# phi(k)v in four groups of 32 columns, with a reordered start and a reordered end of each batch

## The chip, the cores and the metric

One core of one Trainium2 chip runs the whole layer in one launch. The metric is the device time in microseconds (us) of an execution. All rows below come from one profiled execution of the kernel before.

## The reference, cut to what matters

The input x is 16 sequences of 512 tokens with 256 channels. It is normalised, and the output is x + attention(xn) + ffn(xn). The change touches the linear attention:

```python
q, k, v = xn @ Wq + bq, xn @ Wk + bk, xn @ Wv + bv      # 16 heads of 16 channels
q, k = elu(q) + 1, elu(k) + 1                           # phi(q), phi(k)
kv = einsum('bkhd,bkhm->bhdm', k, v)                    # 16 x 16 for each head
out = einsum('bqhd,bhdm->bqhm', q, kv) / maximum(q . sum_k k, 1e-6)
attention = out.reshape(B, S, 256) @ Wo + bo
```

The ffn is a shared SwiGLU of 512 hidden channels plus a SwiGLU whose output goes through the two best of 8 experts of a token.

## The kernel before, in words

Work goes in 16 batches (one sequence each; the first and the last are written out, 1 to 14 are one loop), and then in 75 tiles of 128 tokens that are sorted by pair of experts (the tile stage). Products that need more than one pass are done as three matmuls of rounded high and low parts (mm3, L337 to L339: high*high, high*low, low*high); a matmul that is written once in plain f32 is run by the chip as two pairs of weight load and matmul.

A batch on TensorE (batch, L476): k and v of the four token blocks (L481 to L494), q (L498), hidden(0) of the shared ffn, then **phi(k)v** (L514 to L518), hidden(1), routed(0), the ranks of the tokens (L529, L534), the normalisers (L543), routed(1) and routed(2), the product with Wo (L558), routed(3), spread (L566), hidden(2), hidden(3), and the output sums y (L592 to L608). Waits stand between them by hand: L540 waits for gate(0) of VectorE before the normalisers, L556 for the transposed kv, L569 for the third routed gate, L593 and L600 for the low parts of the hidden values that GpSimd makes.

phi(k)v takes, for each of two chunks c of 128 channels and four token blocks t, phi(k)'s 128 columns as the stationary operand and v's 128 columns with a column of ones behind them as the moving one: 8 products of 128 x 129 of which only the 16 x 16 blocks on the diagonal are wanted. VectorE reads the column of ones as the sum of k (L966), adds bv times that sum (L973), sets all but the heads' blocks to zero with the mask head (L977), and transposes the result within blocks of 32 (L987). It is the stationary operand of L558.

The engines beside TensorE, in the order written out by hand:

- VectorE in a batch (L925): norm(b+1), base(b-1) (which adds y to the residual), k_in for four blocks with normalise(b+1) behind the second, phi_k, the expert choice in some 20 small dependent steps (probabilities, best_two), phi(q) (L960), ksum and khead, gate(0) (L971), kvm, gate(1), the ranks and table rows with routed_gate(0) among them, the transposition, routed_gate(1), the reciprocals (L993 to L1001), routed_gate(2), m_lo, routed_gate(3), qn, gate(2), qn_lo, **x_transposed(b+1, 0)**, gate(3), x_transposed(b+1, 1), t_low(b+1). In the first batch norm(1) stands at L989 and **normalise(1)** at L1006, ahead of routed_gate(2). normalise waits for a power that GpSimd takes (reciprocal_root, L1156). x_transposed waits for the reload of the normalised x (xn_ld) and for the scattered stores of the routed values (hs_st).
- ScalarE: the copy of v out of the accumulator (L689), the exponentials, the silus, the high parts (high, L676), the high part of x (t_high, L667) behind high(3).
- GpSimd: the residual's bias (L1186), the split of 1/16 of the experts' weights, low(0), low(1), four scattered stores of table rows and four of routed values (L1181), low(2), low(3) (L1162).
- SyncE issues the loads and stores; x of batch b+2 is loaded once x_transposed of b+1 is through (L373).

At the start SyncE issues x in four parts, the constants, the weights of k and v (stage_kv), then the rest. ScalarE makes high parts of stage_kv, waits for the weights of q (L734), and only then makes the high part of x (first_high, L736), then those of w_in and half of w1. GpSimd makes the low parts of w_in in cuts of 256 columns (L1234 to L1236), and the parts of w1. In the last batch VectorE also works out the list of tiles (tile_list, L1003), and SyncE stores zeros in 13 places (L409) after ends_rdy (L984) and before the first tile's loads.

Of the kernel before, what the change touches and what calls it, by code (L numbers as in the profile page):

```python
# [6 lines left out]
def layer_program(nc, x, w_k, w_v, w_q, w_o, w_in, w_out, w_exp, w_rt, b_q, b_kl, b_vo,  # L7
# [3 lines left out]
    ALU = mybir.AluOpType  # L11
# [3 lines left out]
    P = 128  # L15
    B, S, D = 16, 512, 256
# [30 lines left out]
    with ctx:  # L47
# [27 lines left out]
        v = sb("v", [P, TB, DC, P + 1], f32)  # L75
# [8 lines left out]
        stay = sb("stay", [P, 2 * P + DC * 32 + NROW + 11], f32)  # L84
        ident = stay[:, 0:P]
        head = stay[:, P:2 * P]
        heads = stay[:, 2 * P:2 * P + DC * 32].rearrange("p (c n) -> p c n", c=DC)
        crow = stay[:, 2 * P + DC * 32:2 * P + DC * 32 + NROW]
        cpart = stay[:, 2 * P + DC * 32 + NROW:]
# [10 lines left out]
        bvo = sb("bvo", [P, 2 * D], f32)  # L100
        bv, bo = bvo[:, 0:D].rearrange("p (c n) -> p c n", c=DC), bvo[:, D:2 * D]
# [9 lines left out]
        kvm = relut[:, 0, 0:DC * P].rearrange("p (c n) -> p c n", c=DC)  # L111
        kvT = relut[:, 1, 0:DC * P].rearrange("p (c n) -> p c n", c=DC)
# [235 lines left out]
        def _(sp):  # L348
# [7 lines left out]
            loads(kv_w_ld, [], stage_kv)  # L356
# [3 lines left out]
            loads(out_w_ld, [(bvo[:, :], b_vo), (wo[:, :, :], w_o)], [])  # L360
# [6 lines left out]
            def load(b, last):  # L367
# [7 lines left out]
                if first_row(b):  # L375
                    sp.wait_ge(ffn_split, 1)
                else:
                    wait_apart(sp, base_rdy, DC * b)
                    sp.dma_start(out_rows(b - 1), res[:, :, :]).then_inc(base_st, 16)
                    wait_apart(sp, base_st, 16 * b)  # L380
                sp.dma_start(res[:, :, :], x_rows(b)).then_inc(r_ld, 16)
                if first_row(b):
                    sp.wait_ge(w1_split, 1)
                    loads(out_w_ld, [], stage_out)
                    sp.wait_ge(ffn_split, 3)
                else:
                    sp.wait_ge(wexp_split, b)
# [51 lines left out]
        def _(pe):  # L439
# [36 lines left out]
            def batch(b, last):  # L476
# [28 lines left out]
                if first_row(b):  # L505
                    pe.wait_ge(ffn_split, 2)
# [81 lines left out]
                if first_row(b):  # L588
                    pe.wait_ge(ffn_split, 3)
# [62 lines left out]
        def _(act):  # L652
# [29 lines left out]
            def batch(b, last):  # L682
# [3 lines left out]
                for i in range(2):  # L686
                    act.wait_ge(v_done, 2 * b + i + 1)
                    wait(act, acc_done, b)
                    act.copy(v[:, 2 * i:2 * i + 2, :, 0:P],  # L689
                             bank[7 if i == 0 else 0][:, :].rearrange("p (t c n) -> p t c n", t=2, c=DC)).then_inc(v_rdy, 1)  # L690
# [6 lines left out]
                    act.activation(expt[:, i, :], expt[:, i, :], ACT.Exp, scale=-1.0).then_inc(ek_rdy, 1)  # L697
                act.wait_ge(lg_rdy, b + 1)
# [78 lines left out]
        def _(dve):  # L777
# [147 lines left out]
            def batch(b, last):  # L925
# [29 lines left out]
                if first_row(b):  # L955
                    dve.wait_ge(ffn_split, 2)
# [4 lines left out]
                acc = bank[2][:, 0:DC * (P + 1)].rearrange("p (c n) -> p c n", c=DC)  # L961
# [4 lines left out]
                dve.tensor_copy(ksum[:, :], acc[:, :, P]).then_inc(kstep, 1)  # L966
# [5 lines left out]
                for c in range(DC):  # L972
                    ins = dve.scalar_tensor_tensor(kvm[:, c, :], bv[:, c, :], ksum[:, c:c + 1], acc[:, c, 0:P],  # L973
# [3 lines left out]
                dve.tensor_tensor(kvm[:, :, :], kvm[:, :, :], head.unsqueeze(1).broadcast_to([P, DC, P]),  # L977
# [9 lines left out]
                dve.transpose(kvT.rearrange("p c n -> p (c n)"), kvm.rearrange("p c n -> p (c n)")).then_inc(kvT_rdy, 1)  # L987
# [17 lines left out]
                if first_row(b):  # L1005
                    normalise(1)  # L1006
# [85 lines left out]
            dve.memset(v[:, :, :, P:P + 1], 1.0)  # L1092
# [54 lines left out]
        def _(pool):  # L1147
# [30 lines left out]
            def batch(b, last):  # L1178
# [21 lines left out]
                if first_row(b):  # L1200
                    pool.wait_ge(out_w_ld, 16 * 3)
                    high_part(wstage[:, :], wout_hi_)
                    pool.wait_ge(pool_set, 4)
# [33 lines left out]
            pool.wait_ge(w1_ld, 16 * 2)  # L1237
            pool.wait_ge(w_round, len(stage_kv) + len(stage_q) + len(stage_in) + 1)
            low_part(stage_w1[0][0], stage_w1[0][2], stage_w1[0][3], w1_split)
            high_part(stage_w1[1][0], stage_w1[1][2])  # L1240
            pool.wait_ge(pool_set, 3)
            low_part(stage_w1[1][0], stage_w1[1][2], stage_w1[1][3], w1_split)
# [34 lines left out]
def constants():  # L1277
# [5 lines left out]
    head = (p[:, None] // 16 == p[None, :] // 16).astype(np.float32)  # L1283
# [62 lines left out]
```

## Time and profile before

| what | us |
|---|---|
| three timed runs: median (lowest to highest) | 950.98 (949.29 to 952.27) |
| the profiled execution, its own time | 949.65 |
| its span, first to last instruction | 947.8 |
| TensorE matmuls busy in the span | 920.9 |
| VectorE, GpSimd, ScalarE busy | 703.4, 471.0, 362.6 |

The span leaves 1.85 us of the execution's time outside it. The profiled execution is 1.3 us below the median of the runs. Batches 1 to 14 repeat with a period of about 43.3 us; the tile stage begins at 723.2 us. Matmuls overlap in their pipeline, so a row's duration is longer than what the matmul costs; the distance between two starts is the cost.

### The profile page before, as it was taken

Reading aid. Unit: us, or ns where it says so; the run is one execution under the profiler, and the core shown is the slowest. Engines: PE = TensorE matmul, PEld = TensorE weight load, DVE = VectorE, ACT = ScalarE, POOL = GpSimd, SP = SyncE. Lnnn points to the kernel's source line nnn. Section 1 sums busy time; section 2 is a strip of 40 time slices with the busy share of each in tenths; the row PEclk is TensorE's granted clock in tenths of the full one; section 3 lists DMA queues with packets and bytes.
Section 4 is the critical chain, followed back from the end, with each engine's and each line's share of the span. In section 5 each row is a group of like instructions: output and inputs, shape, how many; then the busy total and the mean of one; then the engine's idle time right before and its main releaser. Section 6 shows DMA issues by size and latency. Waiting matters only on the chain. (4 is left out here: it accounts for less than half of the span.)

```text
span 947.8 us, 21218 instructions
## 1 busy us (share of the span) xinstructions
PE 920.9 (97%) x6206; PEld 836.3 (88%) x6207; DVE 703.4 (74%) x1770; ACT 362.6 (38%) x595; POOL 471.0 (50%) x550
## 2 busy tenths in 40 slices
PE   7879999999999999999999999999999999999995
PEld 6778989898988989898988889898879999999995
DVE  5768687877878686877778787868495787777773
ACT  4425345353435354453434353544332222222220
POOL 4764453535253543645353534535262656665554
PEclk8989999999999999999999999999999999999998
DMA  9242323241413223232413132231235777787760
GB/s 271 67 125 87 105 72 135 67 122 46 121 67 100 89 78 117 62 134 65 122 56 111 67 100 89 78 129 44 93 132 164 145 144 142 140 147 142 136 128 1
DMA packets 145911, 100.34 MB, mean 106 GB/s; under 512 B 55520, under 2 KB 136800, under 8 KB 145888
## 3 DMA queue, kind: packets, MB, share of 16 engines
q1 hardware_dynamic: 106032, 64.76, 23.8%
q0 software_dynamic: 17968, 25.32, 12.3%
q10 hardware_dynamic: 21888, 9.97, 3.8%
q8 instruction: 12, 0.20, 0.1%
q14 instruction: 11, 0.09, 0.0%
HBM read 53.43 MB, written 48.00 MB: 107 GB/s over the span
## 5 line engine op out<-in xcount | busy, mean ns | idle before, releaser
L337 PE MATMUL bank<-wexp_hi,xnT_hi 128*128 (+1 forms) x560 | 190.9, 341 | 0.0
L339 PE MATMUL bank<-wexp_hi,xnT_lo 128*128 (+1 forms) x560 | 186.2, 332 | 0.0
L338 PE MATMUL bank<-wexp_lo,xnT_hi 128*128 (+1 forms) x560 | 185.8, 332 | 0.0
L1162 POOL TENSOR_TENSOR h_lo<-gated,h_hi 128x256 fp32r<-128x256 f32 x128 | 100.6, 805 | 124.9 <-ACT h_hi L676 124.9
L337 PEld LDWEIGHTS bank<-wexp_hi,xnT_hi 128*128 128x128 f32 x560 | 106.2, 190 | 13.1 <-issue 3.2
L339 PEld LDWEIGHTS bank<-wexp_hi,xnT_lo 128*128 128x128 f32 x560 | 106.2, 190 | 10.4
L338 PEld LDWEIGHTS bank<-wexp_lo,xnT_hi 128*128 128x128 f32 x560 | 106.3, 190 | 9.6
L337 PE MATMUL bank<-xnT_hi,win_hi 128*128 128x512 f32 x256 | 102.0, 398 | 8.5 <-DVE expt L923 8.5
L1186 POOL TENSOR_TENSOR res<-res,bvo 128x256 f32<-128x256 f32 x64 | 48.3, 785 | 115.3 <-DMA res<-x 115.3
L339 PE MATMUL bank<-xnT_hi,win_lo 128*128 128x512 f32 x256 | 100.5, 393 | 0.0
L338 PE MATMUL bank<-xnT_lo,win_hi 128*128 128x512 f32 x256 | 100.3, 392 | 0.0
L676 ACT CAST h_hi<-gated 128x512 fp32r<-128x512 f32 x64 | 39.8, 622 | 116.7 <-DVE gated L919 116.7
L338 PE MATMUL bank<-wexp_lo,h_hi 128*128 x296 | 83.3, 281 | 0.0
L337 PE MATMUL bank<-wexp_hi,h_hi 128*128 x296 | 83.1, 281 | 0.0
L1181 POOL DMA_INDIRECT tab_d<-rows,pos_i x64 | 64.2, 1003 | 37.9 <-DVE tok L915 21.3
L339 PE MATMUL bank<-wexp_hi,h_lo 128*128 x296 | 83.0, 281 | 0.0
L1259 POOL DMA_INDIRECT out<-res,idx_cur x39 | 61.5, 1577 | 39.0 <-DVE res L1116 32.0
L337 PE MATMUL bank<-wkv_hi,xnT_hi 128*128 128x266 f32 (+1 forms) x256 | 73.7, 288 | 4.8 <-DVE xnT_lo L824 4.8
L338 PE MATMUL bank<-wkv_lo,xnT_hi 128*128 128x266 f32 (+1 forms) x256 | 73.5, 287 | 0.0
L339 PE MATMUL bank<-wkv_hi,xnT_lo 128*128 128x266 f32 (+1 forms) x256 | 73.2, 286 | 0.0
L339 PE MATMUL bank<-wout_hi,h_lo 128*128 128x256 f32 x256 | 72.2, 282 | 0.0
L337 PE MATMUL bank<-wout_hi,h_hi 128*128 128x256 f32 x256 | 72.2, 282 | 0.0
(190 smaller groups left out, 2433.8 us busy)
## 6 DMA issues: line engine op xcount, KB each, us to landing
res<-x SPq DMA_DIRECT2D x16, 512.0 KB, 3.6
out<-res SPq DMA_DIRECT2D x16, 512.0 KB, 2.9
xt<-x SPq DMA_DIRECT2D x15, 512.0 KB, 3.5
xn_d<-xt SPq DMA_DIRECT2D x15, 512.0 KB, 4.8
xt<-xn_d SPq DMA_DIRECT2D x60, 128.0 KB, 3.2
xt<-h_d SPq DMA_DIRECT2D x76, 64.0 KB
xt<-h_d ACTq DMA_DIRECT2D x76, 64.0 KB
kb<-h_d SPq DMA_DIRECT2D x76, 64.0 KB
```

The costliest lines, as they stand in the source:

```text
L337: e.matmul(to, w_hi, m_hi_, start=first_, stop=False, skip_group_check=free)
L338: e.matmul(to, w_hi, m_lo_, start=False, stop=False, skip_group_check=free)
L339: return e.matmul(to, w_lo, m_hi_, start=False, stop=last_, skip_group_check=free)
L676: act.copy(h_hi[:, j, :], gated[:, j % 2, :]).then_inc(hhi_rdy, 1)
L1162: ins = pool.tensor_tensor(h_lo[:, j, cols], gated[:, j % 2, cols], h_hi[:, j, cols].bitcast(f32), ALU.subtract)
L1181: pool.indirect_dma_start(d, bass.IndirectOffsetOnAxis(ap=pos_i[:, t:t + 1], axis=0), src, None).then_inc(done, 16)
L1186: ins = pool.tensor_tensor(res[:, t, :], res[:, t, :], bo, ALU.add)
L1259: pool.indirect_dma_start(out, bass.IndirectOffsetOnAxis(ap=idx_cur[:, t // TB, t % TB:t % TB + 1], axis=0), ring[t], None, bounds_check=N ...
```

## The change

It makes phi(k)v of 4 times as many matmuls of a quarter of the width. The stationary operand is 32 columns of phi(k) (two heads), the moving one the same 32 columns of v and a column of ones, and the four groups of a chunk go to the four blocks of 32 partitions of the accumulator. kvm is then 32 wide, kvT is a tile of its own that is zero outside its diagonal blocks, and four transpositions of 32 partitions fill these. Beside that:

- the bias bv comes with the constants in the new layout, and b_vo becomes b_o;
- the weights of k and v are issued from ScalarE's queue at the start, and first_high stands ahead of the wait for q's weights;
- both high parts of w1 are made by ScalarE inside the first batch, between the exponentials of k and those of q; GpSimd makes only low parts, w_in's in cuts of 128 columns, in the order in which hidden(0) to hidden(3) need them;
- in the first batch, normalise(1) stands behind qn instead of ahead of routed_gate(2);
- in each batch, gate(3) stands ahead of both halves of x_transposed.

```diff
-        v = sb("v", [P, TB, DC, P + 1], f32)
+        v = sb("v", [P, TB, DC, QG, HP + 1], f32)          # HP = 32, QG = 4
-        kvm = relut[:, 0, 0:DC * P].rearrange("p (c n) -> p c n", c=DC)
-        kvT = relut[:, 1, 0:DC * P].rearrange("p (c n) -> p c n", c=DC)
+        kvm = relut[:, 0, 0:DC * HP].rearrange("p (c n) -> p c n", c=DC)
+        kvT = sb("kvT", [P, DC, P], f32)
...
             sp.dma_start(stay[:, :], c_stay).then_inc(stay_ld, 16)
-            loads(kv_w_ld, [], stage_kv)
...
                 if first_row(b):
-                    pe.wait_ge(ffn_split, 2)
+                    pe.wait_ge(ffn_split, 1)
...
                 for c in range(DC):
                     for t in range(TB):
-                        mm = pe.matmul(bank[2][:, c * (P + 1):(c + 1) * (P + 1)], phik[:, t, c * P:(c + 1) * P], v[:, t, c, :],
-                                       start=(c == 0 and t == 0), stop=(t == TB - 1), skip_group_check=True)
+                        for n in range(QG):
+                            at = c * P + n * HP
+                            mm = pe.matmul(bank[2][n * HP:(n + 1) * HP, c * (HP + 1):(c + 1) * (HP + 1)], phik[:, t, at:at + HP],
+                                           v[:, t, c, n, :], start=(c == 0 and t == 0), stop=(t == TB - 1), skip_group_check=True)
                 mm.then_inc(acc_done, 1)
+                if first_row(b):
+                    pe.wait_ge(ffn_split, 2)
                 hidden(1, (0, 1))
...
-                    act.copy(v[:, 2 * i:2 * i + 2, :, 0:P],
-                             bank[7 if i == 0 else 0][:, :].rearrange("p (t c n) -> p t c n", t=2, c=DC)).then_inc(v_rdy, 1)
+                    act.copy(v[:, 2 * i:2 * i + 2, :, :, 0:HP].rearrange("p t c h n -> p (t c h) n"),
+                             bank[7 if i == 0 else 0][:, :].rearrange("p (o n) -> p o n", n=HP)).then_inc(v_rdy, 1)
...
+                if first_row(b):
+                    act.wait_ge(w1_ld, 16 * 2)
+                    high_parts(stage_w1)
                 act.wait_ge(lg_rdy, b + 1)
...
+            for buf, of, _, _ in stage_kv:
+                act.dma_start(buf, of).then_inc(kv_w_ld, 16)
             act.wait_ge(kv_w_ld, 16 * 3)
             high_parts(stage_kv)
+            first_high()
             act.wait_ge(q_w_ld, 16 * 4)
             high_parts(stage_q)
-            first_high()
             act.wait_ge(in_w_ld, 16 * 2)
             high_parts(stage_in)
-            act.wait_ge(w1_ld, 16 * 2)
-            high_parts(stage_w1[:1])
...
-                    ins = dve.scalar_tensor_tensor(kvm[:, c, :], bv[:, c, :], ksum[:, c:c + 1], acc[:, c, 0:P],
+                    ins = dve.scalar_tensor_tensor(kvm[:, c, :], bv[:, c, :], ksum[:, c:c + 1], acc[:, c, 0:HP],
...
-                dve.transpose(kvT.rearrange("p c n -> p (c n)"), kvm.rearrange("p c n -> p (c n)")).then_inc(kvT_rdy, 1)
+                wait(dve, m_done, b)
+                for i in range(4):
+                    rows = slice(HP * i, HP * i + HP)
+                    ins = dve.transpose(kvT[rows, :, HP * i:HP * i + HP], kvm[rows, :, :])
+                ins.then_inc(kvT_rdy, 1)
...
                 if last:
                     tile_list()
-                if first_row(b):
-                    normalise(1)
                 routed_gate(b, 2, 1)
...
                     dve.tensor_tensor(qn[:, c, :], phiq[:, c, :], bank[(6, 2)[c]][:, :], ALU.mult).then_inc(qn_rdy, 1)
+                if first_row(b):
+                    normalise(1)
                 gate(b, 2, 1)
...
+                gate(b, 3, 7)
                 if not last:
                     x_transposed(b + 1, 0)
-                gate(b, 3, 7)
-                if not last:
                     x_transposed(b + 1, 1)
                     t_low(b + 1)
...
+            dve.memset(kvT[:, :, :], 0.0)
...
-            for n, (buf, _, hi, lo) in enumerate(stage_in):
-                pool.wait_ge(w_round, len(stage_kv) + len(stage_q) + n + 1)
-                low_part(buf, hi, lo, ffn_split)
...
+            pool.wait_ge(w_round, first + len(stage_in))
+            for j in range(HC):
+                for buf, _, hi, lo in stage_in:
+                    for at in (j * P, 512 + j * P):
+                        ins = pool.tensor_tensor(lo[:, at:at + P], buf[:, at:at + P], hi[:, at:at + P].bitcast(f32), ALU.subtract)
+                ins.then_inc(ffn_split, 1)
+            for n in range(2):
+                pool.wait_ge(w_round, first + len(stage_in) + n + 1)
+                low_part(stage_w1[n][0], stage_w1[n][2], stage_w1[n][3], w1_split)
```

## Rows read from the trace of the kernel before

**Rows 1.** The page, busy time of each engine.
```profile
PE 920.9 (97%) x6206; PEld 836.3 (88%) x6207; DVE 703.4 (74%) x1770; ACT 362.6 (38%) x595; POOL 471.0 (50%) x550
```

**Rows 2.** Timeline of TensorE around phi(k)v: start us, us, engine line op
```profile
295.90 1.95 PE L516 MATMUL bank<-v,phik 128*128 128x129 f32 x16
297.60 0.48 PE L337 MATMUL bank<-xnT_hi,win_hi 128*128 128x512 f32 x1
297.92 0.40 PE L338 MATMUL bank<-xnT_lo,win_hi 128*128 128x512 f32 x1
298.15 0.39 PE L339 MATMUL bank<-xnT_hi,win_lo 128*128 128x512 f32 x1
```

**Rows 3.** The same view around the normalisers.
```profile
303.44 0.65 PE L543 MATMUL bank<-phiq,khead 128*32 128x128 f32 x16
304.02 0.50 PE L337 MATMUL bank<-wexp_hi,xnT_hi 128*128 128x512 f32 x1
304.35 0.39 PE L338 MATMUL bank<-wexp_lo,xnT_hi 128*128 128x512 f32 x1
```

**Rows 4.** L543 in short windows: start:end us, length, PE and PEld busy (instructions), clock
```profile
303.44:303.48 0.04, 0.04 (x4) 0.04 (x6) 1.00 0.00 0
303.48:303.57 0.09, 0.09 (x4) 0.09 (x8) 1.00 0.00 0
```

**Rows 5.** Line views of TensorE's queue, one batch: when its sequencer was at L547, L550
```profile
L547 PEldq ALU_OP  x1: 32/32/32, 303.5 to 303.5; - x1
L550 PEldq ALU_OP  x1: 32/32/32, 303.7 to 303.7; - x1
```

**Rows 6.** Timeline of VectorE, same batch: fourth k_in and gate(0)
```profile
289.92 0.42 DVE L930 TENSOR_TENSOR kb<-bank,bkl 128x256 f32<-128x256 f32 x1 [0.73 <-PE bank L339]
301.85 0.68 DVE L919 TENSOR_TENSOR gated<-gated,bank 128x512 f32<-128x512 f32 x1
```

**Rows 7.** Timelines of VectorE, GpSimd and TensorE at the end of that batch.
```profile
319.96 0.71 DVE L830 STREAM_TRANSPOSE phik<-xt 128x512 f32<-128x512 f32 x1 [0.79 <-DMA h_d<-expt,pos_i]
320.60 0.65 DVE L919 TENSOR_TENSOR gated<-gated,bank 128x512 f32<-128x512 f32 x1
321.98 1.44 POOL L1162 TENSOR_TENSOR h_lo<-gated,h_hi 128x256 fp32r<-128x256 f32 x2 [1.52 <-ACT h_hi L676]
323.31 0.28 PE L339 MATMUL bank<-wout_hi,h_lo 128*128 128x256 f32 x1
323.56 0.36 PE L337 MATMUL bank<-m_hi,qn_hi 128*128 128x256 f32 x1
323.76 0.28 PE L338 MATMUL bank<-m_lo,qn_hi 128*128 128x256 f32 x1
```

**Rows 8.** Who waited for whom: us in total, times, longest
```profile
PE bank L337 <- POOL h_lo L1162: 2.6, 2, 1.8
```

**Rows 9.** Batch 14: timeline of VectorE; a window of all engines (clock 0.50)
```profile
668.32 0.71 DVE L830 STREAM_TRANSPOSE phik<-xt 128x512 f32<-128x512 f32 x1 [2.68 <-DMA h_d<-expt,pos_i]
672.30:675.70 3.40, 3.40 (x18) 3.40 (x17) 0.60 (x1) 0.00 (x0) 0.00 (x0) 0.50 0.00 0
```

**Rows 10.** The start: timelines of ScalarE and TensorE.
```profile
11.33 0.62 ACT L655 CAST wq_hi<-expt 128x512 fp32r<-128x512 f32 x1 [2.15 <-DMA relut<-c_round]
13.30 0.56 PE L337 MATMUL bank<-wkv_hi,xnT_hi 128*128 128x266 f32 x1 [4.75 <-DVE xnT_lo L824]
```

**Rows 11.** Batches 0 and 1: timelines of VectorE and TensorE.
```profile
47.92 3.02 DVE L818 TENSOR_SCALAR xt<-xt,mv,rstd 128x256 f32<-128x256 f32 x4 [4.49 <-POOL rstd L1156]
51.59 0.80 PE L337 MATMUL bank<-xnT_hi,win_hi 128*128 128x512 f32 x1 [7.15 <-DVE expt L923]
59.66 0.71 DVE L830 STREAM_TRANSPOSE phik<-xt 128x512 f32<-128x512 f32 x1 [1.14 <-DMA xt<-xn_d]
```

**Rows 12.** The last batch: SyncE's zeros, the first tile's low part.
```profile
698.66 13.97 SPq L409 DMA_DIRECT2D h_d<-wstage  x13
722.36 0.65 DVE L1089 TENSOR_TENSOR xnT_lo<-phiq,xnT_hi 128x512 fp32r<-128x512 f32 x1
```

More of the change, by code:

```diff
@@ L15, in layer_program @@
     P = 128
+    HP = 32
+    QG = P // HP
     B, S, D = 16, 512, 256
@@ L83, in layer_program @@
         NROW = 16 + 4 * NSLOT
-        stay = sb("stay", [P, 2 * P + DC * 32 + NROW + 11], f32)
+        stay = sb("stay", [P, P + 3 * HP + DC * 32 + NROW + 11], f32)
         ident = stay[:, 0:P]
[L86 to L89, printed above, removed]
+        head = stay[:, P:P + HP]
+        bv = stay[:, P + HP:P + 3 * HP].rearrange("p (c n) -> p c n", c=DC)
+        stay_at = P + 3 * HP
+        heads = stay[:, stay_at:stay_at + DC * 32].rearrange("p (c n) -> p c n", c=DC)
+        crow = stay[:, stay_at + DC * 32:stay_at + DC * 32 + NROW]
+        cpart = stay[:, stay_at + DC * 32 + NROW:]
         triones = sb("triones", [P, 2, P], bf16)
@@ L99, in layer_program @@
         bk, brt = bkl[:, 0:D], bkl[:, D:KL]
-        bvo = sb("bvo", [P, 2 * D], f32)
-        bv, bo = bvo[:, 0:D].rearrange("p (c n) -> p c n", c=DC), bvo[:, D:2 * D]
+        bo_t = sb("bo_t", [P, D], f32)
+        bo = bo_t[:, :]
         stats = sb("stats", [P, TB, 6], f32)
@@ L359, in _ @@
             loads(w1_ld, [], stage_w1)
-            loads(out_w_ld, [(bvo[:, :], b_vo), (wo[:, :, :], w_o)], [])
+            loads(out_w_ld, [(bo, b_o), (wo[:, :, :], w_o)], [])
             sp.wait_ge(fill_set, 2)
@@ L375, in load @@
                 if first_row(b):
-                    sp.wait_ge(ffn_split, 1)
+                    sp.wait_ge(ffn_split, HC)
                 else:
@@ L384, in load @@
                     loads(out_w_ld, [], stage_out)
-                    sp.wait_ge(ffn_split, 3)
+                    sp.wait_ge(ffn_split, HC + 1)
                 else:
@@ L588, in batch @@
                 if first_row(b):
-                    pe.wait_ge(ffn_split, 3)
+                    pe.wait_ge(ffn_split, HC + 1)
                 if last:
@@ L955, in batch @@
                 if first_row(b):
-                    dve.wait_ge(ffn_split, 2)
+                    dve.wait_ge(ffn_split, HC)
                 for o in range(DC):
@@ L965, in batch @@
                 dve.wait_ge(acc_done, b + 1)
-                dve.tensor_copy(ksum[:, :], acc[:, :, P]).then_inc(kstep, 1)
+                dve.tensor_copy(ksum[:, :], acc[:, :, HP]).then_inc(kstep, 1)
                 dve.wait_ge(kstep, KS * b + 1)
@@ L976, in batch @@
                 dve.wait_ge(kstep, KS * b + 3)
-                dve.tensor_tensor(kvm[:, :, :], kvm[:, :, :], head.unsqueeze(1).broadcast_to([P, DC, P]),
+                dve.tensor_tensor(kvm[:, :, :], kvm[:, :, :], head.unsqueeze(1).broadcast_to([P, DC, HP]),
                                   ALU.mult).then_inc(kvm_rdy, 1)
@@ L1202, in batch @@
                     high_part(wstage[:, :], wout_hi_)
-                    pool.wait_ge(pool_set, 4)
+                    pool.wait_ge(pool_set, 3)
                     low_part(wstage[:, :], wout_hi_, wout_lo_, ffn_split)
@@ L1232, in high_part @@
                 ins.then_inc(pool_set, 1)
-            for n, (buf, _, hi, lo) in enumerate(stage_in):
-                pool.wait_ge(w_round, len(stage_kv) + len(stage_q) + n + 1)
-                low_part(buf, hi, lo, ffn_split)
[L1237 to L1242, printed above, removed]
+            first = len(stage_kv) + len(stage_q)
+            pool.wait_ge(w_round, first + len(stage_in))
[7 more added lines that the diff above has]
+                low_part(stage_w1[n][0], stage_w1[n][2], stage_w1[n][3], w1_split)
             wout_hi_, wout_lo_ = (w[:, :, :].rearrange("p c n -> p (c n)") for w in (wout_hi, wout_lo))
@@ L1274, in _, with constants @@
                 pool.wait_ge(out_st[t], 16 * (NG if t < LAST_TILES else NG - 1))
-def constants():
+def constants(bv):
     P, D, N = 128, 256, 8192
@@ L1297, in constants @@
     part = np.stack([p * P, p] + [t * P + p for t in range(4)] + [-(p // 16 % 2)] + [p // 32 == t for t in range(4)], 1)
-    stay = np.concatenate([ident, head, heads.reshape(P, -1), crow, part], 1)
+    bv = np.repeat(bv.reshape(2, 4, 32).transpose(1, 0, 2).reshape(4, 64), 32, 0)
+    stay = np.concatenate([ident, head, bv, heads.reshape(P, -1), crow, part], 1)
     other = np.concatenate([tri, spread.reshape(P, -1)], 1)
@@ L1335 @@
         "b_kl": every(np.concatenate([a["L0_attn_bk"], a["L0_ffn_gb"], a["L0_ffn_eb"]])),
-        "b_vo": every(np.concatenate([a["L0_attn_bv"], a["L0_attn_bo"]])),
-        **constants(),
+        "b_o": every(a["L0_attn_bo"]),
+        **constants(a["L0_attn_bv"]),
     }
```

8 lines of the change are left out of this document (4 added, 4 removed).

## The prediction

> **What bounds the kernel now.** I read first the busy times: TensorE's matmuls cover 920.9 of 947.8 us, no other engine is above 74% [rows 1]. Then TensorE's own waits: where its stalls are few and long, a gain comes either from fewer matmul slots or from those few stalls [rows 8, 10, 11]. Then the timelines around phi(k)v and around the normalisers, because L543 is already a product in four groups of 32 columns and so prices the new form [rows 2 to 4]. Last VectorE's order, since an edit that makes TensorE faster runs into what VectorE delivers to it [rows 6, 7]. A slot is the distance between two starts, not a row's duration: an f32r matmul of 512 columns costs 0.23 us (297.92 to 298.15), one of 256 columns 0.12 (323.76 follows 323.56 by more, of which below).
>
> **Part 1, phi(k)v on TensorE.** Old cost: 16 pairs of load and matmul start at 295.90; the second matmul behind them starts at 297.92. That is 2.02 us, less 0.23 for the first one behind: 1.79 us in a batch, 0.11 for each pair [rows 2].
>
> New: 64 pairs of 32 stationary and 33 moving columns. L543 is 16 pairs of 32 and 128: from 303.44 to the second matmul behind at 304.35, less 0.23, is 0.68 us [rows 3]. Inside it four matmuls start within 0.04 us, then none until after 303.57 [rows 4]: the four groups run side by side, a round of four every 0.11 us, which is 256 columns (two passes of 128) at the granted full clock. Four rounds are 0.44, so leaving the mode costs 0.68 - 0.44 = 0.24, and I add 0.11, one exposed load, for entering it. With 33 columns a round is 33/128 of 0.109, 0.028 us; 16 rounds are 0.45. Floor: 0.11 + 0.45 + 0.24 = 0.80 us.
>
> The question is whether pairs come that fast (7 ns each). The queue's own rows bound it: TensorE's sequencer was at L547 at 303.5 and at L550 at 303.7, and between these lines stand the 12 pairs of routed(1) [rows 5]. So it hands over a pair in at most 17 ns. Before phi(k)v it stands some 16 pairs ahead (in those rows 12 of L543's 16 were still to start). The other 48 at 17 ns are 0.82 us: at most 0.11 + 0.82 + 0.24 = 1.17. The group saves G = 0.62 to 0.99 us.
>
> VectorE caps that. From the start of its fourth k_in, 289.92, it is busy nearly without a pause until gate(0) ends at 302.53, and none of those steps changes [rows 6]. L543 waits for gate(0) and starts at 303.44 [rows 3]; with 0.14 us from an engine's end to the matmul it releases (GpSimd's 323.42 to 323.56 [rows 7]) it can start at 302.67, 0.77 earlier and not more. I take 0.75 a batch, nearest to the cap because both ends of G straddle it. It counts from batch 1's k to batch 15's k, 14 times: **-10.5 us**. Bounds 0.35 (twice the supply time I allow) to 0.80: -5 to -11.
>
> In batch 15 the next stage hangs on VectorE: ends_rdy, then 13 stores of zeros over 13.97 us, then the first tile's loads, whose low part ends at 723.01 as TensorE arrives [rows 12]. phi(k)v is not in that path; I count 0.
>
> The copy of v, the narrower kvm and mask, and four small transpositions for one of 0.44 us stand outside the path (kvT's next reader is L558, behind routed(2)). I cost them at nothing; their cover is TensorE's routed(1) and routed(2), and if it went, the four transpositions would cost some 0.1 us a batch.
>
> **Part 2, gate(3) ahead of x_transposed.** VectorE waits for the scattered stores until 319.96, transposes, and starts gate(3) only at 320.60. Behind gate(3) come ScalarE's high(3) and GpSimd's low(3), which ends at 323.42; TensorE starts the last part of y at 323.56 where 323.43 was its slot, and the pair behind is 0.20 away, not 0.12: 0.45 us for two slots of 0.12 [rows 7]. The stall is 0.21 us in each batch. With gate(3) 0.6 us earlier it goes: 13 batches x 0.21 = **-2.7 us**. What is late next is low(2), on GpSimd behind the eight scattered stores. The transpositions end when they did, or 0.6 earlier, since gate(3) no longer lies between them.
>
> In batch 14 the stores come late, VectorE waits 2.68 us for them with gate(3) behind, TensorE stalls 1.8 us by the wait's row and 2.0 by the starts [rows 8, 9], and the clock is then at its lower level from 672.3 to 675.7, which costs half of 3.4 us [rows 9]. Both should go: -3.7; **-3.5 us** taken, since low(2) may be late too. Bounds -1.5 to -3.7.
>
> **Part 3, the start and batches 0 and 1.** TensorE waits 4.75 us for the low part of x [rows 10]. In that chain ScalarE waits 2.15 us for the load that ends q's group and makes q's high part, 0.5, ahead of x's. That goes: 2.6 us. Against it, 522 KB of weights of k and v now share the DMA engines with x's 512 KB from the first microsecond on, and x heads the chain. No row shows the mix; bounds are a gain of 4.75 (the whole wait) and a loss of 1. I take 2.0, the removed 2.6 less some delay of x.
>
> In batch 0 TensorE waits 7.15 us for routed_gate(2) behind normalise(1), which waits for GpSimd until 47.9 and takes 3.02 us [rows 11]; the clock is lower behind it (the row's 0.80 us against the usual 0.39). Moved behind qn, normalise(1) frees that gate, but it still ends at 50.9 less the start's gain, and the store and reload of the normalised x, x_transposed (59.66, waiting for the reload [rows 11]), the load of the next x, norm(2), base(0) and k_in(0) of batch 1 follow in one chain that knows nothing of TensorE. So most of the 7.15 comes back as waits for GpSimd's low parts in batch 0 and for k_in in batch 1. What stays: 2.0 of the start, 0.6 from gate(3) leaving the two transpositions, and what VectorE waited for TensorE ahead of two of batch 1's four k_in, twice about 0.73 (as [rows 6] shows for a later batch): 4.1. Some 0.6 more I take for base(0), which no longer waits for y. **-4.7 us**, bounds -2 to -7.5. Those of w1's high parts that ScalarE now makes inside batch 0 delay q's exponentials by 2 us; VectorE has the expert choice to do meanwhile.
>
> **Sum.** 10.5 + 2.7 + 3.5 + 4.7 = 21.4. Against the profiled execution's 949.65 that gives 928.3; the median of the runs stands 1.3 higher, so 929.5.
>
> **A rule against the change.** Rows: matmuls of different column groups start four in 0.04 us [rows 4]. TensorEngine Tiling (Array Packing), Instruction Overhead, in the Trainium skill says that a matmul has some 60 cycles of overhead, so that one column costs what 60 do, and that no factor should be taken from a dimension already small; 33 columns are below that. By it, as an estimate, 64 times 25 ns are 1.6 us and the group would cost 1.95, more than now. The rows of L543 do not show such a floor across groups.
>
> **Rivals.** *A, supply binds (slower).* The queue holds enough for L543's 16 pairs, so its burst may say little of 64. Place: the 48 pairs behind the first 16. If they came no faster than the slowest spacing of small pairs in these rows that isn't set by their columns, L516's own 0.11 us, the group would cost 0.35 + 64 x 0.11 = 7.4, +5.6 a batch; at 0.06 us, +2.4 a batch over 16 batches is +38, less 11 of parts 2 and 3: 978. It turns the total to slower by 0.3% above about 0.036 us a pair. For: nothing in the trace keeps up small pairs for long. Against: 17 ns between L547 and L550. TensorE: Matmul & The Clock Gate (What happens when you issue a matmul) in the Trainium skill gives 62 ns for each matmul where the sequencer's program decodes; the rows of L547 and L550 speak against it here.
>
> *B, the groups load one after another (small gain).* If 64 loads of 32 columns queue up at a quarter of L516's 0.107 us each, the group costs 0.35 + 1.71 = 2.06, +0.27 in 16 batches: 949.65 + 4.3 - 10.9 + 1.3 = 944. Against: the six loads within 0.04 us [rows 4].
>
> *C, the gain in phi(k)v is there, but parts 2 and 3 give nothing.* If x's loads are delayed as much as the wait for q saved, and batch 0's stall only moves, the time is 949.65 - 10.5 - 2.7 + 1.3 = 938.
>
> *D, nothing measurable:* the group half fast (1.8 us) and C together, about 948 to 951.
>
> **Chances.** Forecast 0.62, C 0.16, B 0.08, D 0.05, A 0.09. A measurement can tell about 0.3% (2.9 us) from no change. A and its like are slower: 0.09; D is mostly the same, 0.05; the rest faster, 0.86. Range: the forecast's terms at their bounds give 926 to 940 (5 + 2.7 + 1.5 + 2 = 11.2 less at the weak end, 11 + 2.7 + 3.7 + 7.5 = 24.9 at the strong one); this takes C in. I give 923 to 941.
>
> **What would show it.** Right: L516 as 64 narrow pairs within 0.5 to 0.9 us and the second matmul behind at 0.8 to 1.2 less one slot; L543 starting some 0.14 us after gate(0) ends; no stall ahead of the last part of y and none in batch 14; a period of 42.3 to 42.4 us; the first k matmul near 11.3; no wait of 7 us in batch 0 but shorter ones at low(3) of batch 0 and at batch 1's second k_in. Wrong: starts of L516 more than 0.03 us apart, a period above 43, or a first k matmul at 13 or later.

## The result and the profile after

| | before | after |
|---|---|---|
| median of four runs each, us | 950.44 | 935.94 |
| lowest to highest | 949.29 to 952.27 | 934.71 to 937.40 |
| the profiled execution, its span | 949.65, 947.8 | 936.16, 934.3 |

The ratio is 0.9846 [0.9824, 0.9868]: faster, by 14.5 us or 1.5%. The forecast was 929.5 with a range of 923 to 941. The sign and the range hold; the sum of the steps was 21.4 us, and the profiled executions differ by 13.5.

The clearest clock in these traces is the first matmul of phi(k)v in each batch. It stands at these times, in us from the start of the span (L516 before, L521 after):

| | batch 0 | batch 1 | each of the 13 steps from batch 1 to 14 | from batch 14 to 15 | batch 15 | from there to the end of the span |
|---|---|---|---|---|---|---|
| before | 26.31 | 79.35 | 43.3 | 46.69 | 689.06 | 258.7 |
| after | 25.23 | 77.19 | 42.3 to 42.7 | 42.69 | 671.69 | 262.6 |
| gained | 1.1 | 2.2 | 0.86 a batch | 4.0 | 17.4 | -3.9 |

So 17.4 us were gained up to batch 15 (2.2, then 13 times 0.86, then 4.0), and 3.9 of them were lost behind it. First the page's busy times and TensorE's own waits (us in total, times, longest), to set beside [rows 1, 8]:

```profile
PE 907.5 (97%) x6974; PEld 818.6 (88%) x6975; DVE 697.6 (75%) x1819; ACT 363.4 (39%) x596; POOL 464.9 (50%) x554
```

```profile
PE bank L341 <- POOL h_lo L1176: 3.7, 1, 3.7
PE bank L341 <- DVE expt L933: 3.1, 1, 3.1
PE bank L449 <- DVE phik L821: 2.5, 1, 2.5
PE bank L341 <- DVE phik L933: 1.6, 1, 1.6
PE bank L341 <- DVE xnT_lo L834: 1.3, 1, 1.3
```

TensorE's matmuls are busy 13.4 us less, as much as the span is shorter. The two stalls behind the last low part are now one of 3.7 us, in batch 0. The one of 3.1 us stands in the last batch, where it was 1.3 before.

Then TensorE's timeline around phi(k)v and the normalisers, against [rows 2, 3], with VectorE's steps between them, against [rows 6]:

```profile
289.31 0.39 PE L343 MATMUL bank<-xnT_hi,win_lo 128*128 128x512 f32 x1
289.63 0.77 PE L521 MATMUL bank<-v,phik 128*32 128x33 f32 x64
290.32 0.50 PE L341 MATMUL bank<-xnT_hi,win_hi 128*128 128x512 f32 x1
290.66 0.39 PE L342 MATMUL bank<-xnT_lo,win_hi 128*128 128x512 f32 x1
...
296.32 0.64 PE L550 MATMUL bank<-phiq,khead 128*32 128x128 f32 x16
```

```profile
283.53 0.42 DVE L940 TENSOR_TENSOR kb<-bank,bkl 128x256 f32<-128x256 f32 x1 [0.72 <-PE bank L343]
...
295.50 0.68 DVE L929 TENSOR_TENSOR gated<-gated,bank 128x512 f32<-128x512 f32 x1
```

From 289.63 to the second matmul behind, 290.66, less 0.23, is 0.80 us for 64 pairs: the floor of the forecast to the hundredth. The hundredth is luck. A window over the group shows that all 64 pairs are started within 0.58 us, 9 ns apart and not the 7 of the floor:

```profile
289.62:290.21 0.59, 0.58 (x64) 0.58 (x64) 1.00 0.59 138
```

And what it costs to enter the form of four column groups, which the floor counts inside (0.11), stands ahead of the first start: 0.32 us behind the start before it (289.31), where a slot is 0.23. With that the group costs 0.89, and the change saves TensorE 0.90 us a batch, not 0.99. gate(0) ends at 296.18 and the normalisers start 0.14 later, as forecast. From the fourth k_in to the normalisers is 12.79 us where it was 13.52: 0.73 gained, 0.75 forecast.

Last the two ends that go against the forecast. The start, from ScalarE and TensorE [rows 10]; batches 0 and 1 [rows 11]; the last batch [rows 12]:

```profile
10.69 1.07 ACT L667 CAST xnT_hi<-bank 128x512 fp32r<-128x512 f32 x2 [3.70 <-PE bank L449]
12.15 0.56 PE L341 MATMUL bank<-wkv_hi,xnT_hi 128*128 128x266 f32 x1 [1.28 <-DVE xnT_lo L834]
```

```profile
41.70 0.50 PE L341 MATMUL bank<-wexp_hi,xnT_hi 128*128 128x512 f32 x1 [1.64 <-DVE phik L933]
57.20 0.58 PE L341 MATMUL bank<-wout_hi,h_hi 128*128 128x256 f32 x1 [3.67 <-POOL h_lo L1176]
60.47 1.30 DVE L840 STREAM_TRANSPOSE phik<-xt 128x512 f32<-128x512 f32 x2 [7.45 <-DMA h_d<-expt,pos_i]
69.35 0.38 PE L341 MATMUL bank<-wkv_hi,xnT_hi 128*128 128x256 f32 x1 [1.21 <-DVE lg L941]
```

```profile
681.77 13.66 SPq L412 DMA_DIRECT2D h_d<-wstage  x13
683.21 0.99 DVE L1000 STREAM_TRANSPOSE kvT<-relut 32x64 f32<-32x64 f32 x4
691.80 0.79 PE L341 MATMUL bank<-xnT_hi,win_hi 128*128 128x512 f32 x1 [3.12 <-DVE expt L933]
699.01 0.21 DVE L1037 CAST info_i<-bank 1x76 int32<-1x76 f32 x1
699.80 0.88 SPq L348 DMA_DIRECT2D xt<-h_d  x2
```

The last batch's stall in the kernel before, and the one in the tile stage of the changed kernel, where before there was none:

```profile
708.35 0.50 PE L337 MATMUL bank<-xnT_hi,win_hi 128*128 128x512 f32 x1 [1.32 <-DVE expt L923]
720.79 0.38 PE L341 MATMUL bank<-wexp_hi,xnT_hi 128*128 x1 [0.67 <-DVE xnT_lo L1102]
```

The wait for x's low part is 1.28 us instead of 4.75, but the first K matmul comes only 1.15 earlier: TensorE has waited before it, for the normalised x, since x's four loads take 3.5 us from issue to landing (2.3 in start_back, below, which keeps the old order). In batch 0 the wait of 7.15 us is gone. Of it there are now 3.7 at the last low part and 1.2 in batch 1. The 1.6 at routed_gate(1) are new too, but belong to phi(k)v in four groups: they stand in regroup_only (1.7, below), which keeps the old places of the rest. VectorE transposes the next x at 60.47, later than before [rows 11], for it waits 7.45 us for the scattered stores. In the last batch TensorE stands 3.1 us behind the list of tiles, and the granted clock behind that stall is at its lower level (0.50 from 691.7 to 695.0).

### The profile page after: what moved, and what is told of

Its sections match the earlier page's. It is cut to its first block and busy times, and to the rows that moved or that the text cites. A ratio compares the mean times of both kernels' runs of the same rounds, so it can differ in the third digit from the quotient of the medians.

```text
span 934.3 us, 22822 instructions
## 1 busy us (share of the span) xinstructions
PE 907.5 (97%) x6974; PEld 818.6 (88%) x6975; DVE 697.6 (75%) x1819; ACT 363.4 (39%) x596; POOL 464.9 (50%) x554
## 5 line engine op out<-in xcount | busy, mean ns | idle before, releaser
L1176 POOL TENSOR_TENSOR h_lo<-gated,h_hi 128x256 fp32r<-128x256 f32 x128 | 97.1, 779 | 104.0 <-ACT h_hi L683 103.6
L1200 POOL TENSOR_TENSOR res<-res,bo_t 128x256 f32<-128x256 f32 x64 | 47.2, 766 | 113.5 <-DMA res<-x 113.5
L929 DVE TENSOR_TENSOR gated<-gated,bank 128x512 f32<-128x512 f32 x64 | 43.9, 685 | 43.7 <-ACT gated L679 43.7
```

Source lines behind the costliest of these rows:

```text
L929: dve.tensor_tensor(gated[:, j % 2, :], gated[:, j % 2, :], bank[up_bank][:, :], ALU.mult).then_inc(gate_rdy, 1)
L1176: ins = pool.tensor_tensor(h_lo[:, j, cols], gated[:, j % 2, cols], h_hi[:, j, cols].bitcast(f32), ALU.subtract)
L1200: ins = pool.tensor_tensor(res[:, t, :], res[:, t, :], bo, ALU.add)
```

## The experiments

The comparison of two traces leaves one thing open: which part of the change shortened the period. The forecast gave 0.75 us a batch to phi(k)v and 0.21 to the order of gate(3), and added them.

**One part alone, and one part undone.** regroup_only keeps the new phi(k)v with its constants, mask and transpositions and takes back all the rest:

```diff
+            loads(kv_w_ld, [], stage_kv)
...
-            for buf, of, _, _ in stage_kv:
-                act.dma_start(buf, of).then_inc(kv_w_ld, 16)
...
-            first_high()
             act.wait_ge(q_w_ld, 16 * 4)
             high_parts(stage_q)
+            first_high()
...
-                gate(b, 3, 7)
                 if not last:
                     x_transposed(b + 1, 0)
+                gate(b, 3, 7)
+                if not last:
                     x_transposed(b + 1, 1)
```

The casts and normalise(1) go back as in casts_back and norm1_back below.

> The kernel before with nothing but phi(k) v in four groups (constants, mask and transposes with it). Theory: the regrouping is worth 0.73 us in each period of the batches, as much as the wait of the normalisers for gate(0) leaves, and gives 0.5 to 2 us back in the last batch, where the four transposes stand bare and TensorE waits behind the tile list: 950.4 less 9 to 10.5, so 940 to 941.5 us. Rival: the order of VectorE at the end of a batch carried the period, the regrouping alone is hidden as its end just waits longer: 946 us or more.

It took 950.31 us, 1.0007 [0.9997, 1.0017] of the kernel before. Alone, phi(k)v in half of the time gave **nothing** in the whole: the theory missed by 9 us, and the rival (946 or more) stands. Up to batch 15 its trace is 2.6 us ahead of the kernel before, and it loses 3.4 behind it. gate3_back is the changed kernel with the last part of that diff alone:

> The changed kernel with the first half of the next x's transposition back ahead of gate(3). Theory: 0.1 to 0.2 us a batch come back at the wait for GpSimd's last low part, and batch 14 gets back its stall and its half clock of some 2 to 3.5 us: 935.9 plus 3.5 to 6, so 939.5 to 942 us. Rival: batch 14's gain came from the shorter phi(k) v, and the order of gate(3) is worth the 0.1 us a batch alone: 937 to 938 us.

It took 953.95 us, 1.0050 [1.0034, 1.0067]: the place of one line costs 18 us against the changed kernel. Theory and rival both fell; 10.1 us of it stand in the 13 steady steps, 2.3 in batch 14 and 4.4 in batch 0, where gate(3) now stands behind a wait of 7.9 us for the scattered stores. And gate3_only is the kernel before with nothing but that line moved:

> The kernel before with nothing but gate(3) ahead of both halves of the transposition. The runs so far showed that the regrouping alone gives nothing and that the changed kernel without this order is back at 952 us. Theory: the kernel before has two loops of nearly the same length, TensorE's own slots (some 43.1 us a batch) and the one through GpSimd's scattered stores, the transposition, gate(3) and the last low part (43.25 us); with gate(3) ahead only the first is left, so the period falls from 43.32 to 43.1 us and batch 14 from 46.7 to 43.2: 950.2 less 6, 944 us (942.5 to 946). Rival: the order carries the 1.1 us a batch which its removal cost in the changed kernel: 932 to 935.

It took 946.74 us, 0.9942 [0.9928, 0.9956], in a set of runs whose kernel before stood at 951.84: 5.1 us, near the theory's 6. Its step from batch 14 to 15 is 43.27 us, 3.4 less than before. The steps of phi(k)v's starts in the steady batches make the table by which all three are read:

| step, us | gate(3) between the transpositions | gate(3) ahead |
|---|---|---|
| phi(k)v of 128 columns | 43.31 (before) | 43.11 (gate3_only, one of 44.18 aside) |
| phi(k)v in four groups | 43.2 (regroup_only, gate3_back) | 42.45 (after) |

Either part alone is worth 0.1 to 0.2 us a batch, both together 0.86. (gate3_only comes from a slower set of runs, of which below; its 43.11 may be a little high.) That is what two loops of nearly equal length do: the longer one sets the period, and an edit that shortens one of them leaves the other. Here is one turn of the second, in regroup_only, from VectorE's fourth k_in of a batch to that of the next, out of the timelines of VectorE, GpSimd and TensorE:

```profile
289.59 0.42 DVE L936 TENSOR_TENSOR kb<-bank,bkl 128x256 f32<-128x256 f32 x1 [0.72 <-PE bank L343]
306.82 0.17 DVE L921 TENSOR_SCALAR tok<-tok 128x4 f32<-128x4 f32 x1
307.81 1.05 POOL L1192 DMA_INDIRECT tab_d<-rows,pos_i  x1 [1.41 <-DVE tok L921]
...
316.75 0.96 POOL L1192 DMA_INDIRECT h_d<-expt,pos_i  x1 [0.30 <-issue]
319.56 0.71 DVE L836 STREAM_TRANSPOSE phik<-xt 128x512 f32<-128x512 f32 x1 [1.47 <-DMA h_d<-expt,pos_i]
320.19 0.65 DVE L925 TENSOR_TENSOR gated<-gated,bank 128x512 f32<-128x512 f32 x1
321.57 1.42 POOL L1173 TENSOR_TENSOR h_lo<-gated,h_hi 128x256 fp32r<-128x256 f32 x2 [2.19 <-ACT h_hi L682]
323.14 0.36 PE L341 MATMUL bank<-m_hi,qn_hi 128*128 128x256 f32 x1 [0.56 <-POOL h_lo L1173]
332.82 0.42 DVE L936 TENSOR_TENSOR kb<-bank,bkl 128x256 f32<-128x256 f32 x1 [0.72 <-PE bank L343]
```

Downwards, from start to start: 17.2 us of VectorE's steps to the last of the table rows, 1.0 to the first scattered store on GpSimd, 8.9 from there to the eighth, 2.8 from that one to the moment VectorE may transpose, 3.6 through gate(3), high(3) and low(3), and 9.7 us of TensorE's y and k: 43.2. phi(k)v is nowhere in it. The kernel before has the same distances (17.2, 1.0, 9.0 and 2.8), so this loop set its period too. In the changed kernel the same turn has gate(3) no longer behind the stores:

```profile
283.53 0.42 DVE L940 TENSOR_TENSOR kb<-bank,bkl 128x256 f32<-128x256 f32 x1 [0.72 <-PE bank L343]
300.76 0.17 DVE L925 TENSOR_SCALAR tok<-tok 128x4 f32<-128x4 f32 x1
312.88 0.69 DVE L929 TENSOR_TENSOR gated<-gated,bank 128x512 f32<-128x512 f32 x1 [0.84 <-ACT gated L679]
313.52 1.30 DVE L840 STREAM_TRANSPOSE phik<-xt 128x512 f32<-128x512 f32 x2
314.29 1.44 POOL L1176 TENSOR_TENSOR h_lo<-gated,h_hi 128x256 fp32r<-128x256 f32 x2 [0.96 <-ACT h_hi L683]
326.00 0.42 DVE L940 TENSOR_TENSOR kb<-bank,bkl 128x256 f32<-128x256 f32 x1 [0.72 <-PE bank L343]
```

From k_in to gate(3) it is 29.35 us instead of 30.60, and the transposition finds the stores landed. The waits say the same, regroup_only's of TensorE and of VectorE, and VectorE's of the kernel before:

```profile
PE bank L341 <- POOL h_lo L1173: 9.6, 15, 2.2
DVE phik L836 <- DMA h_d<-expt,pos_i: 22.3, 14, 3.4
DVE phik L830 <- DMA h_d<-expt,pos_i: 12.9, 14, 2.7
```

Each batch's gain of 0.75 us went into these: VectorE waits 1.6 us a batch for the stores, where it was 0.9 (12.9 over 14), and TensorE waits in 15 places for the last low part where [rows 8] have two. In gate3_back it is 17.6 us in 16 places.

**The groups side by side.** outer_n turns the loops, so that the 16 matmuls of one column group come in a row:

```diff
-                for c in range(DC):
-                    for t in range(TB):
-                        for n in range(QG):
+                for n in range(QG):
+                    for c in range(DC):
+                        for t in range(TB):
```

> The changed kernel with the loops of phi(k) v turned, so that the 16 matmuls of one column group follow one another. Theory: the 64 pairs take 0.80 us only since neighbours lie in different groups and run side by side; in one group each waits for the one before, 50 ns or more a pair, 3.2 us or more for the group, +2.4 us in each of 16 batches: 974 us or more. Rival: the pairs are paced by how fast they are handed over, whatever group they are in: 936.

951.27 us, 0.9998 [0.9985, 1.0010], and a step of 43.49 us:

```profile
294.93 1.92 PE L521 MATMUL bank<-v,phik 128*32 128x33 f32 x64
296.78 0.50 PE L341 MATMUL bank<-xnT_hi,win_hi 128*128 128x512 f32 x1
297.12 0.39 PE L342 MATMUL bank<-xnT_lo,win_hi 128*128 128x512 f32 x1
```

2.19 less 0.23 is 1.96 us, against 0.80 with neighbours in different groups: 1.16 more in each batch. The order decides, as the theory said, but its size was wrong: the 64 starts lie 27 ns apart in the mean, not 50, and the step is 1.04 us longer than the changed kernel's 42.45. This set of runs was a slower one, of which below; against the changed kernel in another such set (42.81 us a step, 0.9862) it is 0.7 us a batch, and some 13 us in all.

Why 27 ns? [rows 2] have 0.11 us for a pair of 129 columns in one group, and 33/129 of that is 0.028: the columns alone explain it. The rule that was weighed in the prediction comes near too. TensorEngine Tiling (Array Packing), Instruction Overhead, in the Trainium skill has some 60 cycles of overhead for a matmul, from which the prediction's estimate was 25 ns a start and 1.95 us for the group. No run here has fewer columns, so these can't be told apart, and 1.96 does not show the rule. The changed kernel does speak against it across groups: its 64 starts lie 9 ns apart.

**The start and batch 0.** start_back puts the loads of the weights of k and v back on SyncE and x's high parts behind q's cast:

```diff
+            loads(kv_w_ld, [], stage_kv)
...
-            first_high()
             act.wait_ge(q_w_ld, 16 * 4)
             high_parts(stage_q)
+            first_high()
```

> The changed kernel with the key and value weights loaded from SyncE behind x, and the first x's high parts behind the query weights' casts, as before. Theory: the first K matmul starts 1.1 us later (13.3 us from the span's start), but the gain does not reach batch 1, which waits for the chain over GpSimd and the stores: +0.3 to 0.8 us, 936.2 to 936.8. Rival, the prediction's: the whole of the earlier start reaches the end, +1.1 to 2 us, 937 to 938.

937.48 us, 0.9869 [0.9853, 0.9884]. The first K matmul came at 13.95 (13.3 expected), behind a wait of 5.3 us, and batch 1's phi(k)v at 79.86, 2.7 us later than in the changed kernel. So the start's gain did reach batch 1, against my theory; 1.3 of the 2.7 us were left in the span. The rival's +1.1 to +2 us fits, with 1.5, though that interval and the changed kernel's overlap; what carries the reading is the trace. casts_back takes back the order of ScalarE's and GpSimd's casts:

```diff
-                if first_row(b):
-                    act.wait_ge(w1_ld, 16 * 2)
-                    high_parts(stage_w1)
...
+            act.wait_ge(w1_ld, 16 * 2)
+            high_parts(stage_w1[:1])
```

The first hunk stands inside batch 0, the second ahead of it; GpSimd makes w_in's low parts by whole chunks again, and w1's second high part.

> The changed kernel with the casts and splits of the expert and feed-forward weights back in the old order: one cast of ScalarE ahead of batch 0 and none inside it, GpSimd's low parts by whole chunks. Theory: the two casts inside batch 0 hold back ScalarE's exponentials of the logits by 1.3 us, and so gate(0) and GpSimd's chain, but GpSimd's old order holds hidden(0) longer; the two nearly cancel: -0.5 to +1 us. Rival, the prediction's: the new order is worth its whole 1.5 us or more: 937.5 us or more.

934.98 us, 0.9848 [0.9833, 0.9864], with batch 1's phi(k)v at 76.38: that part of the change is worth nothing here, and the old order may be a little better (0.8 us by that start, too small for the times to show). norm1_back puts normalise(1) back ahead of routed_gate(2):

```diff
                 if last:
                     tile_list()
+                if first_row(b):
+                    normalise(1)
                 routed_gate(b, 2, 1)
...
-                if first_row(b):
-                    normalise(1)
                 gate(b, 2, 1)
```

> The changed kernel with normalise(1) of batch 0 back ahead of routed_gate(2). Theory: the stall of some 6 us at hidden(2) of batch 0 comes back, with its half clock, but the waits of 3.7 us for the low part and of 1.2 us in batch 1 go, so that it costs 1 to 2 us: the move was worth no more than that. Rival, the reading of a clean gain: 4 us or more.

942.42 us against 940.03 of the changed kernel in the same set of runs, 0.9885 [0.9869, 0.9902] against 0.9862 [0.9846, 0.9879]. In its trace a stall stands at hidden(2) of batch 0, and batch 1's phi(k)v comes 2.6 us later than in the control:

```profile
51.39 0.80 PE L341 MATMUL bank<-xnT_hi,win_hi 128*128 128x512 f32 x1 [5.91 <-DVE expt L933]
```

Of 5.9 us removed, 2.4 reach the end: more than the theory's 1 to 2, less than the rival's 4. The two intervals overlap a little, but the traces agree with the 2.4: batch 1 is 2.6 us later.

**Another start, and the list of tiles.** kv_on_sp is the changed kernel with only the first line of start_back's diff (and without ScalarE's loads); tile_late moves the list of tiles:

```diff
-                if last:
-                    tile_list()
                 routed_gate(b, 2, 1)
...
                 routed_gate(b, 3, 7)
+                if last:
+                    tile_list()
```

Its three matmuls stand behind hidden(3), and VectorE's copies of them ahead of gate(2).

> The changed kernel with the weights of k and v loaded from SyncE behind x, but x's high parts still ahead of the query weights' cast. Theory: x lands 1.2 us earlier, since it no longer shares the DMA engines (2.3 against 3.5 us from issue to landing), and the first K matmul starts near 11.2 us instead of 12.15; some of it is lost before batch 1, as batch 1 waits for stores and reload: -0.3 to -0.9 us, 935.0 to 935.6. Rival: the weights of k and v, which land later, hold the start as much: first K matmul at 12.5 or later, 936 to 937.

> The changed kernel with the list of tiles behind routed_gate(3) in VectorE's order of the last batch, and TensorE's three small matmuls on it behind hidden(3). Theory: the stall of 3.1 us and the half clock behind it (4 us of stretch, 1.7 us more) go; the first tile then waits for its loads, which wait for the stores of zeros, so that of 4.8 us some 2 to 3 reach the end: 933 to 934 us. Rival: the tile stage is bound by the stores of zeros and the loads alone: 935.5 to 936.5.

They took 941.58 and 944.61 us, 0.9898 [0.9881, 0.9915] and 0.9923 [0.9909, 0.9937]: both slower than the changed kernel's 0.9846, and both theories seemed to fall. In kv_on_sp x's loads landed in 2.3 us and the first K matmul came at 10.89, as its theory had it; the rest did not follow. But tile_late's trace differs from batch 1 on, where its code is the changed kernel's. So I ran that kernel again, with kernels that combine the edits (casts_kv: casts_back and kv_on_sp; casts_kv_tile: tile_late on top).

> The changed kernel once more, unchanged, as the control. In the four runs of the last call the thirteen stores of zeros took 16.6 to 17.5 us, in all kernels before them 13.5 to 14.0, though no kernel touches them. Theory: that chip serves such things more slowly, and kernels whose TensorE waits for the last low parts pay for it, so that kv_on_sp and tile_late can't be set against the 0.985 of the changed kernel there. If this run falls on such a chip (stores above 16 us), its ratio is 0.989 to 0.991, as kv_on_sp's; on the other kind 0.984 to 0.986. Rival: kv_on_sp and tile_late are slower of themselves, and this run stands at 0.985 wherever it runs.

> The changed kernel with the old order of casts and with the weights of k and v on SyncE behind x. Theory: the first K matmul starts at 10.9 us instead of 12.15, and batch 0 loses 1.1 us less than in the changed kernel; together 1.5 to 2 us below the changed kernel of the same call. Rival: the start's gain is lost at the wait for the stores in batch 0, as part of it was already: the same within 0.7 us.

> The kernel casts_kv with the list of tiles behind routed_gate(3) as in tile_late. Theory: where the stores of zeros take 13.5 us, the tile loads are issued 2 us earlier and the kernel is 1.5 to 2.5 us below casts_kv; where they take 17 us, they end last and it is the same. Rival: the tile stage's own waits take it back anywhere: within 0.7 us of casts_kv.

| one set of runs, before at 952.64 | us | ratio |
|---|---|---|
| after_again | 940.03 | 0.9862 [0.9846, 0.9879] |
| casts_kv | 938.78 | 0.9857 [0.9839, 0.9875] |
| casts_kv_tile | 939.68 | 0.9866 [0.9849, 0.9884] |

The thirteen stores of zeros, in after_again, casts_kv_tile and tile_late, and the tile's first load in casts_kv_tile:

```profile
686.24 16.48 SPq L412 DMA_DIRECT2D h_d<-wstage  x13
```

```profile
684.70 17.31 SPq L413 DMA_DIRECT2D h_d<-wstage  x13
705.01 0.89 SPq L348 DMA_DIRECT2D xt<-h_d  x2
```

```profile
687.98 17.51 SPq L412 DMA_DIRECT2D h_d<-wstage  x13
```

The control's stores took 16.5 us, not the 13.66 above, and its steps were 42.6 to 43.2 us: in that set of runs the conditions were slower for the same program. By its ratio, though, my theory of the control fell: 0.989 lies outside the interval of 0.9862, and the rival's 0.985 inside. The set before it has no run of the changed kernel. Its kernels show the same signs: the thirteen stores took 17.2 us in gate3_only, 16.6 in outer_n and 17.5 in tile_late, and the mean steady step was 42.95 us in tile_late, against 42.81 in the control and 42.45 in the first trace, with the same code in those batches. So kv_on_sp and tile_late can't be set against 0.9846, and whether they are slower of themselves stays open. Against the control, casts_kv is 1.25 us faster with overlapping intervals: its first K matmul came at 10.81 us instead of 11.99, but batch 1's phi(k)v at 77.19 against 76.99, so what the start gave was gone one batch later, as the rival said. casts_kv_tile is no faster than casts_kv: TensorE's stall behind the list is halved, but the tile's loads are issued at 705.0 either way (705.3 in casts_kv), behind the stores of zeros. Whether the later list pays where those stores take 13.7 us was not tried. No version beat the changed kernel by more than the measurement can tell.

## Why the prediction was right, and where it was not

**phi(k)v's own cost, and gate(0) as its cap: right.** 0.80 us for the group (0.80 to 1.17 forecast), or 0.89 with what stands ahead of its first start, and 0.73 gained at the normalisers (0.75). The terms inside the 0.80 were off in both directions; since gate(0) caps the gain, it made no difference.

**Part 1 as a term of its own: wrong in its attribution.** "It counts from batch 1's k to batch 15's k, 14 times: -10.5" would have been only some -1.4 in the steady steps without part 2, and nothing at the end (regroup_only). The step that failed is the cover: I read the wait of 0.79 us for the stores in [rows 7] as what delays gate(3) by 0.6, priced the delay at TensorE's present stall of 0.21, and did not ask what becomes of it when TensorE arrives 0.75 earlier. The loop over the stores had 0.1 us of room. The sum survived because both parts were in the change, and that is luck as far as part 1 goes: 0.86 us in each of the 13 steady steps, against 0.75 + 0.21. Part 2's own term of 0.21 a batch is what gate3_only shows (0.20).

**Batch 14: right.** 4.0 us for the step, against 0.75 + 3.5, and 3.4 of them in gate3_only alone; its stall and its low clock are gone (granted clock 1.00 from 655 to 665).

**Part 3: mis-sized.** -2.2 us at batch 1, -4.7 forecast (bounds -2 to -7.5). The first K matmul came 1.15 us earlier, not 2.0, since x landed later beside the weights; with these on SyncE behind x again it came at 10.89 (kv_on_sp). What I took as kept behind it, base(0)'s 0.6 and the two waits of 0.73, did not come: GpSimd's stores of batch 0 hardly moved (the last was issued at 54.75, before at 54.84), and VectorE waited 7.45 us for them. That most of the 7.15 us would come back as waits for low(3) and at batch 1's k_in was right, in place and in kind (3.7 and 1.2).

**The last batch: the main miss.** "I count 0"; it was 3.9 us of loss. TensorE reached the tile stage 36.4 us after phi(k)v's start, not 34.1, though the batch had 0.9 us less of work. Behind the list of tiles it stalled 3.1 us instead of 1.3, the clock was at its lower level for 3.3 us of work behind it, and the four transpositions stood ahead of the list with 0.99 us instead of 0.44. Costed at nothing with "if it went, some 0.1 us a batch" they were 0.55, where nothing covered them. Of the stall's growth of 1.8 us 0.9 is only TensorE arriving earlier; what makes the batch longer is the 0.55 and, for the most part, the clock: 3.3 us of work at its lower level cost 1.6. casts_kv has the same stall (3.2) without the lower level and reached the tile stage after 35.4 us. regroup_only shows the changed kernel's 36.4, so it is part 1's price and not the reordering's, as far as these traces tell (gate3_only, without part 1 but in a slower set of runs, shows 35.3).

Some 1.5 us more were lost inside the tile stage, 0.67 of them in the one wait at 720.79, for the low part of a tile's x. start_back, casts_back, kv_on_sp and casts_kv, without such a wait, lose 0.1 to 0.6 there against the kernel before, the other kernels 0.9 to 1.8. Why the wait comes in some and not in others stays open.

**Where the 7.9 us went.** 21.4 were forecast and 13.5 measured between the profiled executions: 3.9 are the last batch and the tile stage, 2.5 part 3, and 1.5 the steps from batch 1 to 15 (16.7 forecast, 15.2 measured).

**The rivals.** A, B and D did not come. C (938), the gain in phi(k)v with little from parts 2 and 3, is nearer in time than the forecast, for the wrong reason: without part 2 there is no gain at all.

## What to carry to other kernels

Before a saving on one engine is multiplied by the number of turns, add up the other loop: from one fixed event to the same event in the next turn, through stores, waits and the small steps behind them, leaving out the work that is made shorter. If that sum is shorter than the period by less than the saving, the saving needs a second edit, and the two are worth what neither is worth alone. For narrow matmuls, let neighbours in the order lie in different column groups. And cost small steps once more at the last turn, where what covered them is missing.

## What the runs showed of the hardware that I had not expected

- 64 f32 pairs of 32 by 33 columns took 0.80 us with neighbours in different column groups (starts 9 ns apart in the mean), 1.96 us with the same pairs in the order of the groups (27 ns). Entering that form cost 0.09 us ahead of the first start.
- Four transpositions of 32 partitions by 64 columns took 0.99 us, where one of 128 by 256 took 0.44.
- The same program had steps of 42.3 to 42.7 us in one set of runs and of 42.6 to 43.2 in another, and its thirteen stores took 13.66 and 16.48 us. The changed kernel's median rose by 0.44%, that of the kernel before by 0.23%. In the slower sets ScalarE's silu(2) started later: in tile_late 3.8 us behind the first matmul of hidden(2) (480.42), in the changed kernel's first trace 2.9 (476.23), in the same batch (rows below). That only a kernel without slack on that path pays for it is not shown. Whether it is the chip or its condition these runs can't say.

```profile
484.20 0.60 ACT L678 ACTIVATE gated<-bank 128x512 f32<-128x512 f32 x1 [0.88 <-PE bank L343]
```

```profile
479.16 0.60 ACT L679 ACTIVATE gated<-bank 128x512 f32<-128x512 f32 x1
```
